# Two-layer block on one core of Trainium2: which stretch each sorted expert mixture runs in

## The reference

```python
x = L0_attn_encoding                                   # 4 x 1024 x 128
xn = _layernorm(x, axis=-1)
x = x + _L0_attn_ref(xn, R) + _L0_ffn_ref(xn, ...)     # causal attention; 16 experts, top 2, one shared
xn = _layernorm(x, axis=-1)
x = x + _L1_attn_ref(xn, ...) + _L1_ffn_ref(xn, ...)
# in _L1_ffn_ref:
    x = x + o @ w_up                                   # o: causal attention, 16 heads of 4
    t = _rmsnorm(x, g2).reshape(-1, D)
    probs = jax.nn.softmax(t @ router_w, axis=-1)
    vals, idx = jax.lax.top_k(probs, K)                # K = 2 of E = 8
    hid = jax.nn.silu(einsum('td,edf->tef', t, w1)) * einsum('td,edf->tef', t, w3)   # F = 256
    y_e = einsum('tef,efd->ted', hid, w2)
    return res + einsum('ted,te->td', y_e, gate)
```

## Time and profile before

| | us |
|---|---|
| median of 3 runs | 1955.24 |
| lowest and highest | 1952.80, 1961.43 |
| the profiled execution | 1952.12 |
| its span, first to last instruction | 1950.3 |
| PE busy in it | 1787.3 (92%) |
| DVE busy | 1328.4 (68%) |
| ACT busy | 1213.0 (62%) |
| POOL busy | 357.6 (18%) |

### The profile page before, as it was taken

How to read it: one execution, slowest core, us unless ns; L and a number is a source line. 1 busy time by engine, 2 the same in 40 slices (tenths; PEclk the granted TensorE clock), 3 DMA queues, 4 the chain that set the end, 5 groups by cost and what they waited for, 6 DMA issues and landing times.

```text
span 1950.3 us, 36843 instructions
## 1 busy us (share of the span) xinstructions
PE 1787.3 (92%) x13857; PEld 814.8 (42%) x13947; DVE 1328.4 (68%) x1896; ACT 1213.0 (62%) x2344; POOL 357.6 (18%) x656
## 2 busy tenths in 40 slices
PE   6989899998988899998978999999879999999898
PEld 3664322344554222344654522234445422244455
DVE  6758698784679788783647498877255498785222
ACT  2352578878541678887622578788755677888521
POOL 2002200000042000000033311200055333220044
PEclk9999999999899899998988999999989999999799
DMA  6233510110064010100174201100065111110021
GB/s 201 73 116 90 134 28 18 29 35 3 27 185 120 1 29 18 44 21 2 34 201 111 61 22 41 31 18 20 23 182 134 47 45 47 31 45 4 1 61 38
DMA packets 94161, 115.73 MB, mean 59 GB/s; under 512 B 12952, under 2 KB 51928, under 8 KB 93728
## 3 DMA queue, kind: packets, MB, share of 16 engines
q1 hardware_dynamic: 90912, 107.07, 20.0%
q0 software_dynamic: 3072, 6.30, 1.1%
HBM read 71.67 MB, written 40.86 MB: 58 GB/s over the span
## 4 chain that ended last, share of the span: by engine, by line
PE 49%; DVE 7%; ACT 4%; issue 4%; POOL 2%; DMA 1%; SPq 1%; POOLq 0%; ACTq 0%; DVEq 0%
PE ps L2413 14%; PE ps L2383 12%; PE ps L2340 6%; DVE row_max L1807 3%; PE ps L2504 3%; PE ps L2243 2%; DVE late_max L1807 2%; ACT prob L2032 2%; PE ps L2283 2%; PE ps L2272 2%; PE ps L2521 1%; PE ps L2424 1%; PE ps L2327 1%; POOL sorted_x L1454 1%; PE ps L2510 1%
## 5 line engine op out<-in xcount | busy, mean ns | idle before, releaser
L2032 ACT ACTIVATE prob<-ps 128x512 f32<-128x512 f32 (+1 forms) x1664 | 846.6, 586 | 232.8 <-PE ps L2383 170.8
L1807 DVE TENSOR_REDUCE row_max<-ps 128x2 f32<-128x1024 f32 (+3 forms) x512 | 567.0, 1118 | 165.0 <-PE ps L2340 123.3
L2413 PE MATMUL ps<-prob,v_ones 128*32 128x512 f32 (+3 forms) x4608 | 457.9, 484 | 14.4 <-ACT prob L2032 8.5
L2383 PE MATMUL ps<-q_stack,k_stack 80*128 80x512 bf16 (+5 forms) x1702 | 443.9, 369 | 26.9 <-ACT prob L2032 12.6
L1807 DVE TENSOR_REDUCE late_max<-ps 128x2 f32<-128x1024 f32 (+3 forms) x384 | 415.9, 1083 | 70.1 <-PE ps L2340 40.5
L2340 PE MATMUL ps<-k_stack,q_stack 64*128 64x512 bf16 (+4 forms) x1792 | 306.7, 365 | 34.5 <-DVE row_max L1807 10.3
L2383 PEld LDWEIGHTS ps<-q_stack,k_stack 48*128 48x128 bf16 (+2 forms) x1792 | 117.5, 96 | 350.4 <-ACT prob L2032 241.8
L2340 PEld LDWEIGHTS ps<-k_stack,q_stack 64*128 64x128 bf16 (+1 forms) x1792 | 80.3, 93 | 302.1 <-DVE row_max L1807 115.9
L1967 ACT ACTIVATE prob<-ps 128x512 f32<-128x512 f32 (+1 forms) x86 | 51.2, 596 | 207.8 <-PE ps L2272 197.3
L2413 PEld LDWEIGHTS ps<-prob,v_ones 128*32 128x32 f32 x4608 | 101.9, 110 | 132.2 <-ACT prob L2032 58.1
L2243 PEld LDWEIGHTS ps<-wd,prob 128*128 128x128 f32 (+1 forms) x832 | 108.0, 194 | 51.5 <-issue 40.7
(11 more groups left out here) (234 smaller groups left out, 1747.4 us busy)
## 6 DMA issues: line engine op xcount, KB each, us to landing
spread_w<-scratch_r SPq DMA_DIRECT2D x128, 128.0 KB
k_stack<-scratch_k SPq DMA_DIRECT2D x32, 256.0 KB
q_stack<-scratch_q SPq DMA_DIRECT2D x32, 256.0 KB
scratch_q<-tmp SPq DMA_DIRECT2D x8, 768.0 KB
scratch_k<-tmp SPq DMA_DIRECT2D x8, 768.0 KB
k_stack<-scratch_k SPq DMA_DIRECT2D x96, 64.0 KB
q_stack<-scratch_q SPq DMA_DIRECT2D x96, 64.0 KB
scratch_k<-tmp SPq DMA_DIRECT2D x36, 128.0 KB
```

What stands on the lines that cost most here:

```text
L1807: dve.tensor_reduce((nm_late if lo else nm[G % 2])[:, t, j], both, AX_X, ALU.max).then_inc(s["ring_used"], 1)
L2032: act.activation(to, src, ACT.Exp, scale=SCALES[kind_of(G)]).then_inc(s["p_ready"], 1)
L2383: ins[n] = pe.matmul(dst[n][:, to], with_rest(k_stack, G, head)[:, kc * P:(kc + 1) * P], with_rest(q_stack, G, head)[:, lo:hi], start=k == ...
L2413: ins = pe.matmul(bank(V_BANK)[CW * j:CW * (j + 1), first - at:end - at], v_st[G % 2][:, kc, j, :], p_slot(v, j)[:, first - at:end - at], ...
```

## The change

`SORT_IN` now puts batches 0 and 1 into stretch 3 and batch 2 into the end stretch. Stretch 2 has no sorted mixture. The blocks of batch 2 stand in one `Weave` with the closing of batch 3 and the dense mixture; the dense mixture's first matmuls, first spread and first down matmul wait for the sorted one to be through (they share banks and buffers). Its fetches, mixes and outputs stand on POOL and SP beside the dense steps, each fetch behind one down step, and the spreads of the dense mixture go from POOL to DVE. There are three `sorted_x` and three `sorted_y` buffers, so the waits for a buffer's reuse go, and `clear` issues 18 DMAs and not 12. The scatters are 16 items for the planner and not 8 pairs; batches 0 and 1 keep the wait before each pair.

```diff
-SORT_IN = {2: (0,), 3: (1, 2)}
+SORT_IN = {3: (0, 1), 4: (2,)}
...
-    return "POOL" if which == 1 or b in POOL_FOR and n % C0 < C0 - 1 else "DVE"
+    return "POOL" if which == 0 and b in POOL_FOR and n % C0 < C0 - 1 else "DVE"
...
-            for t in range(T):
-                at = w.op("POOL", ("scatter", b, t), 2.1 if t == 0 or b not in PACED else 4.5, at, lands=2.5 if t == T - 1 else 0.0)
+            for k in range(2 * T):
+                waits = k and k % 2 == 0 and b in PACED
+                at = w.op("POOL", ("scatter", b, k), 3.25 if waits else 1.25, at, lands=0.0 if b in PACED else 1.5)
...
     xT, routed, _, joined, _ = closing(w, B - 1)
+    copied, outs, stored, gated = sorted_mixture(w, B - 2, (), None)
     loads = []
     for n in range(SPREADS):
-        loads.append(spread_in(w, LOADS_OF * plan.mixtures.index((B - 1, 1)) + n, loads, routed))
-    mixture(w, B - 1, 1, xT, routed, (joined, joined), loads)
+        loads.append(spread_in(w, LOADS_OF * plan.mixtures.index((B - 1, 1)) + n, loads, gated))
+    downs = mixture(w, B - 1, 1, xT, routed, (joined, joined), loads, (copied, copied, stored, outs))
+    w.op("SP", ("bring", B - 2), 0.5, copied, lands=2.3)
+    at = stored
+    for k in range(2 * T):
+        at = w.op("POOL", ("fetch", B - 2, k), 1.25, at, downs[k])
+        if k % T == T - 1:
+            at = w.op("POOL", ("mix", B - 2, k // T), 4.6, at)
+            w.op("SP", ("give", B - 2, k // T), 0.5, at, lands=2.3)
...
             def clear():
-                for n in range(2):
+                for n in SORTED:
                     for g in range(SORT_GROUPS):
...
             def scatter(b, k):
+                t, n = divmod(k, 2)
+                if k == 0:
                     pool.wait_ge(s["cleared"], 16 * N_CLEAR)
...
+                elif b in PACED and n == 0:
                     pool.wait_ge(s["scattered"], 16 * 2 * (T * b + t))
...
+                if which == 1 and n == 0:
+                    dve.wait_ge(s["sdown_done"], len(SORTED) * BLOCKS)
...
+                if which == 1 and n == 0:
+                    for g in range(2):
+                        dve.wait_ge(block_stored[g], groups_stored(g, len(SORTED), 0))
...
+                if which == 1 and n == 0:
+                    pe.wait_ge(s["sy_ready"], len(SORTED) * SORT_GROUPS)
...
                         pe.wait_ge(s["tt_ready"], 2 * b + 2)
+                        pe.wait_ge(s["sback_ready"], len(SORTED) * BLOCKS)
```

More of the change, by code:

```diff
@@ L492 @@
 for window, batches in SORT_IN.items():
-    if len(batches) == 1:
-        places = [(n, q) for n in range(3) for q in range(1, 12, 2)]
-        plans = [((0, 0), places, (2, 9), (3, 0), (3, 8))]
-    else:
-        near = [(n, q) for n in range(4) for q in range(1, 12)]
-        plans = [((0, 0), near[:16], (1, 10), (2, 0), (2, 0)), ((2, 1), near[23:], (3, 10), (4, 0), (4, 4))]
+    if window == B:
+        continue
+    near = [(n, q) for n in range(4) for q in range(1, 12)]
+    plans = [((0, 0), near[:16], (1, 10), (2, 0), (2, 0)), ((2, 1), near[23:], (3, 10), (4, 0), (4, 4))]
     for b, (bring, places, first, second, last) in zip(batches, plans):
@@ L695, in mixture @@
                         w.op("SP", ("mixed", b, 1, half), 0.45, out[-1])
+        if which:
+            return downs
         return out, (scaled[-2], scaled[-1], downs[-1], out[-1]), loads
@@ L991, in build @@
         scratch_rest = [nc.dram_tensor(f"scratch_rest{n}", (HEADS * HD, REST, S), BF16).ap() for n in range(2)]
-        sorted_x = [nc.dram_tensor(f"sorted_x{n}", (SLOTS_1, D), F32).ap() for n in range(2)]
-        sorted_y = [nc.dram_tensor(f"sorted_y{n}", (SLOTS_1, D), F32).ap() for n in range(2)]
+        sorted_x = [nc.dram_tensor(f"sorted_x{n}", (SLOTS_1, D), F32).ap() for n in SORTED]
+        sorted_y = [nc.dram_tensor(f"sorted_y{n}", (SLOTS_1, D), F32).ap() for n in SORTED]
         joined_x = [nc.dram_tensor(f"joined_x{b}", (S, D), F32).ap() for b in SORTED]
@@ L1040, in build @@
         N_WEIGHTS = 13
-        N_CLEAR = 2 * SORT_GROUPS
+        N_CLEAR = len(SORTED) * SORT_GROUPS
         N_FILL = 2 + 1 + PARTS
@@ L1442, in place, with scatter @@
                 pool.tensor_copy(expert_at[b][0:1, :], passed[:, :, 0]).then_inc(s["listed"], 1)
-            def scatter(b, t):
-                if t == 0:
+            def scatter(b, k):
+                t, n = divmod(k, 2)
+                if k == 0:
                     pool.wait_ge(s["cleared"], 16 * N_CLEAR)
-                    if b >= 2:
-                        for n in range(2):
-                            pool.wait_ge(block_loaded[n], groups_stored(n, b - 1, 0))
-                elif b in PACED:
+                elif b in PACED and n == 0:
                     pool.wait_ge(s["scattered"], 16 * 2 * (T * b + t))
-                for n in range(2):
-                    to = bass.IndirectOffsetOnAxis(ap=slot_of[b][:, n * T + t:n * T + t + 1], axis=0)
-                    pool.indirect_dma_start(out=sorted_x[b % 2], out_offset=to, in_=t_norm[:, t * D:(t + 1) * D], in_offset=None).then_inc(s["scattered"], 16)
+                to = bass.IndirectOffsetOnAxis(ap=slot_of[b][:, n * T + t:n * T + t + 1], axis=0)
+                pool.indirect_dma_start(out=sorted_x[b], out_offset=to, in_=t_norm[:, t * D:(t + 1) * D], in_offset=None).then_inc(s["scattered"], 16)
             def sort_gate(b, i):
@@ L1467, in fetch @@
             def fetch(b, k):
-                (G, q), (t, choice) = FETCH_AT[b, k], divmod(k, 2)
-                pool.wait_ge(s["pv_done"], QUAD0[G] + q - 1)
+                t, choice = divmod(k, 2)
+                if WINDOW_OF[b] < B:
+                    G, q = FETCH_AT[b, k]
+                    pool.wait_ge(s["pv_done"], QUAD0[G] + q - 1)
+                else:
+                    pool.wait_ge(s["down_done"], plan.step0[B - 1, 1] + k + 1)
                 if k == 0:
@@ L1472, in fetch @@
                         pool.wait_ge(block_stored[n], groups_stored(n, b + 1, 0))
[L1473 to L1474 removed]
+                    pool.wait_ge(s["turned_ready"], min(WINDOW_OF[b], B - 1) + 1)
+                    pool.wait_ge(s["tc_psum"], min(WINDOW_OF[b], B - 1) + 1)
                     if b:
@@ L1478, in fetch @@
                 to = (fetched_0, fetched_1)[choice][:, t * D:(t + 1) * D]
-                pool.indirect_dma_start(out=to, out_offset=None, in_=sorted_y[b % 2], in_offset=at).then_inc(fetched[t * 2 // T], 16)
+                pool.indirect_dma_start(out=to, out_offset=None, in_=sorted_y[b], in_offset=at).then_inc(fetched[t * 2 // T], 16)
             def mix(b, half):
```

11 lines of the change are left out of this document (3 added, 8 removed).

## The result

The changed kernel ran at a median of 1923.96 us (four executions, 1915.33 to 1930.39) beside 1954.99 of the kernel before: a ratio of 0.984, 95% interval 0.981 to 0.988. Measured twice more, it came to 1929.3 us beside 1952.0 (0.9875, 0.984 to 0.991) and to 1929.7 beside 1953.2 (0.988, 0.986 to 0.990). So it is faster, by about 1.2% rather than the 1.6% of the first measurement. The forecast was 1919 us with a range of 1905 to 1935. The range holds; the forecast is 5 us too low by the first measurement and 10 by the later ones, and 1929 us is what rival (a) gave, whose case came true.

What follows compares the result with a forecast made beforehand. TensorE's work plus its holes, with the low clock behind them, was taken as the bound. 1950.3 - 48.8 + 1.0 - 10.0 + 22.8 = 1915.3 us span, 1917.1 with 1.8 around it, plus half of 3.1: 1919, range 1905 to 1935.

Steps and rivals of the forecast that it cites:

- rival (a): Stretch 3 gives nothing, as the loss only moves to where placing ends; 1929 us, chance 0.13.
- Stretch 2, right in kind: Without its sorted mixture, stretch 2 takes the length of its twin, stretch 1: 125.7 against 174.6 us, a gain of 48.8.
- the 9 us above the blocks' own price: In stretch 2, gain beyond 39.5 us of PE work: PE stands 8.9 us behind DVE, then runs at the lower clock.
- Stretch 3, the step that failed: POOL's paired scatters lose PE 13.1 us; as single items they come under cover, and 10 us are gained.
- rival (c): The hole of stretch 3 goes too, since more sorted work stands before it; ten us more, 1909 us, chance 0.09.
- The windows: Window 2 loses sixteen fetches and two mixes on POOL: 1 us longer, bounds -2 and +3; window 3 unchanged.
- The end, right: The end gains a sorted mixture: 145.8 us instead of 123.0, +22.8, bounds +18 and +34; growth over 34 means wrong.
- So that changes nothing: In the end, moving the 1.27 us spreads from POOL to DVE costs nothing, as PE has 2.6 us a step.
- (b): The end runs in series, closing first and blocks behind it: +39.5 us instead of +22.8; 1936 us, chance 0.10.
- (e): In the end the clock stays at 1.2 GHz until the dense mixture runs, doubling 55.6 us; 1975 us, chance 0.04.
- Rival (d): In the end DVE's spreads and POOL's mixes block each other in SBUF; 10.2 us on top, 1929 us, chance 0.04.

Runs made afterwards that it cites:

- placing split: The changed kernel with POOL's placing of each sorted batch in five items, between which products may stand; 1921.7 us (0.986).
- the true landing in all stretches: The changed kernel with placing in five items and the planner told the longer landing of parts and stacks in stretches 1, 2 and 3; 1912.1 us (0.9795).
- spreads on POOL: The changed kernel with the 32 spreads of the dense mixture of layer 1 back on POOL; 1942.6 us (0.996).
- the landing alone: The changed kernel with the planner told, in stretch 3 only, that parts land in 7.0 us and the first stack load takes 5.1; 1919.1 us (0.985).
- both: The changed kernel with placing in five items and the planner told the longer landing in stretch 3; 1913.8 us (0.980), again 1914.4 (0.980).
- the kernel with one mixture in each: The changed kernel with batch 0's sorted mixture back in stretch 2, batch 1's in stretch 3, batch 2's in the end; 1945.6 us (0.996).

## Why the prediction was right, and where it was wrong

The total lies in the range, and faster was right, but the range was wide enough to hold rival (a), and that is the case that came.

**Stretch 2, right in kind, 3 us too high.** -45.5 for -48.8. The twin was a good measure: 129.1 against 126.8 us for stretch 1 of the same execution. Of these 2.2 us one half arises near 1005 us, where the same pairs of up and of gate matmuls take 1.84 and 1.92 us for 1.12 and 1.02 in stretch 1 (mean clock 0.66 from 1003.88 to 1008.88, and 1.00 at the same place of stretch 1), behind the same waits. The other half is at the very end, behind a wait for DVE's spread that both stretches have (3.1 us, and 3.7 in stretch 1). The same sixteen down matmuls take 2.97 us in stretch 1 and 4.08 in stretch 2 (timeline of PE, changed kernel):

```profile
637.54 2.97 PE L2257 MATMUL ps<-wd,prob 128*128 128x128 f32 x16 [3.67 <-DVE prob L1708]
...
1062.71 4.08 PE L2257 MATMUL ps<-wd,prob 128*128 128x128 f32 x16 [3.09 <-DVE prob L1708]
```

In three of the later kernels (placing split, the true landing in all stretches, spreads on POOL) this stretch took 125.9 to 127.2 us at a mean clock of 0.99, in the six others without a mixture there 128.4 to 129.8 at 0.96 to 0.98. What the prediction said of the 9 us above the blocks' own price was half right: the hole was there, came back with the mixture, but taking most of it away gave 2.4 us. Nearly all of the 45 us is busy time of PE (43.3), 3.8 more than 23 blocks take where the clock is 1.00; how to be rid of the lower clock there is open.

**Stretch 3, the step that failed.** Forecast -10, measured +1.4 (+3.9 and +1.0 in the other profiles), the case of rival (a). The step was "in the 37.8 us from 1457.65 to there PE has 10 blocks (17.2), 22 score matmuls (6.6) and two turns of a group (0.9), 24.7 us. So 13.1 us are lost". These are PE's busy times in that piece of the kernel before, and in its first part (view by stretch):

```profile
1457.65:1495.47 37.82, 32.34 (x154) 15.87 (x154) 27.90 (x24) 16.69 (x44) 26.13 (x29) 0.87 0.69 166
1457.65:1468.24 10.59, 8.15 (x27) 2.36 (x27) 8.87 (x8) 1.98 (x6) 8.90 (x10) 0.54 0.64 132
```

and PE's groups of instructions in the whole piece (busy us, mean ns, idle before):

```profile
L2504 PE MATMUL ps<-wgu,spread_w 128*128 x21 | 12.2, 676 | 1.9 <-issue 1.6
L2521 PE MATMUL ps<-wd,prob 128*128 x52 | 8.5, 287 | 0.9 <-ACT prob L2114 0.9
L2510 PE MATMUL ps<-const_f,prob 128*128 128x128 f32 x26 | 5.9, 312 | 0.4 <-POOL prob L1459 0.3
```

PE was busy for 32.3 us, not 24.7. The gates are those of ten blocks (two a block), but the downs are 52, four a block, so thirteen blocks, and 26 transposes back, thirteen too (the 21st gate is the first of batch 2, at the edge): three blocks that had their gates before the hole were finished here. And for 10.6 us the clock was at 0.54, so that 8.2 us of busy time were a little over half that much work at the full clock. So 7.6 of the 13.1 us were busy time, and 5.5 idle; of these 2.0 were waits for row maxima, 1.6 are without a releaser in the profile, 0.9 were for ACT, and POOL caused 0.3 us. The price of a block was right; the count was of one kind of matmul in a piece in whose course the pipeline drained, at the full clock's price. Leaving out half of the scatters confirmed that they did not set the length (0.4 us).

The larger thing was in the shown rows and not drawn from them. In the kernel before, placing runs from 1441.28 to the first scatter at 1457.65, and the wait for the stacks ends in the same moment, within the piece of the earlier trace rows that begins at 1449.80. The prediction put the hole down to the stacks alone, left it "as it is" and had rival (c) take it away by more sorted work ahead. But sorted blocks can't cover a hole that lies over placing, since POOL has to make their products. The four kernels with neither edit, the landing alone, the split alone and both show that: 427.7, 426.8, 427.4 and 414.4 us for stretch and window together.

**The windows.** -1.3 and +0.4, inside -2 to +3, as said; the sixteen fetches and two mixes that window 2 lost had cost it 1.3 us at most.

**The end, right.** +22.1 (22.6 and 22.4 in the other profiles) for +22.8, out of two errors that cancel. The first dense down matmul, which answers to the earlier trace rows:

```profile
1845.90 1.05 PE L2257 MATMUL ps<-wd,prob 128*128 128x128 f32 x8
```

comes 63.4 us after the start of the stretch (60.6 said), and from there to the end it takes 81.6 us (85.2 said). Ahead of it PE was busy for 57.5 us for the 55.6 counted, and the holes sum to 5.9 us for the 5.0 put in. Behind it 5.6 us went where 2 were taken off, and the low clock accounts for no more than 1.7, by which PE's busy time fell (78.0 for 79.7). The other 3.9 are idle time and belong to the spreads' move: 3.4 behind PE's last matmul (7.0 before, 3.6 now), where the drain of POOL no longer ends the program, and about 0.6 of a last wait for a spread. "So that changes nothing", which the prediction said of this move, was wrong: in the new order it is worth 15 us, and without it the end would have grown by 37 us, over the 34 that the prediction named as a sign of being wrong. So the step from 39.5 us of blocks to 22 has two parts: the first down matmul comes 27.7 us later (63.4 for 35.8), since blocks fill the closing's chain, as said, and 5.6 us go behind it. Rivals (b) and (e) did not happen: the weave held, with a mean clock of 0.99.

**Rival (d), DVE against POOL.** It is there, and small. DVE's spreads take 0.69 us; beside the adds of the mixes two of them do not (timelines of DVE and of POOL, changed kernel, the slow ones alone):

```profile
1872.33 1.76 DVE L1708 TENSOR_TENSOR prob<-prob,spread_w 128x512 f32<-128x512 f32 x1 [0.24 <-PE ps L2257]
...
1894.11 1.11 DVE L1708 TENSOR_TENSOR prob<-prob,spread_w 128x512 f32<-128x512 f32 x1 [1.10 <-PE ps L2257]
```

```profile
1872.29 1.27 POOL L1497 TENSOR_TENSOR tmp<-tmp 128x512 f32<-128x512 f32 x1
1873.63 1.60 POOL L1499 TENSOR_TENSOR tmp<-tmp 128x512 f32<-128x512 f32 x1
```

1.07 and 0.42 us of delay, not 10.2, and no wait of PE comes of it. The Trainium skill, page "SBUF — State Buffer", section "Who interferes with whom", says that such a pair of instructions block each other; the trace agrees for these two spreads, and the other way round for an add of 1.80 us on POOL that began at 1891.52, 0.02 us behind the start of a spread that took its usual 0.69. But a spread at 1870.58, beside a multiplication of the same mix, took 0.72 us. So most of the time that both engines were at work cost nothing.

## What to carry to other kernels

Price a stage that is moved by the same stage in its twin places, not by its own work: here the same 39.5 us of matmuls cost 45 us in stretch 2, 29 to 32 in stretch 3, and in the end 22 or 37, by how many holes they fill or open and by which engine the work beside them is on. Before a hole is put down to the one releaser that the waits name, look at what every other engine does in that time; where two causes end together, removing one gives little, and only a run with both removed shows the price. And when the busy time in a piece is counted from instructions, count each kind: a pipeline that drains or fills in the piece makes one kind a wrong measure of the rest.

## What was not expected of the hardware

The parts of the opening, written to DRAM and read again, took 6.9 us from the last write's issue to the first load that waited for it (1411.3 to 1418.2), at a DMA share of 0.73; in stretch 2 of the kernel with one mixture in each the same chain took 5.7 us (990.5 to 996.2), at a share of 1.03. Much of it may be data still on its way: the eight writes carry 4.7 MB, and at the 374 GB/s that the DMAs moved from 1403 to 1413 that is 12.6 us from the first issue at 1402.3, so to 1414.9 (an estimate). No run took the size away. And the lower level of the clock, 1.2 GHz, outlasts its hole by more than the count allowed for: in the kernel before, from 1457.65 on, 0.3 us ahead of the end of a wait of 6.6 us, the granted clock was 0.54 of 2.4 GHz on average for 10.6 us, though PE was busy for 8.2 of them. Last, the drain of 9.2 us behind POOL's last instruction: it cost 3.4 us at the end of the program where POOL worked to the last, and nothing in the changed kernel, where POOL's last mix ended 33 us before the end.
